# Layer three's mask added by GpSimd for six heads of sixteen, and a ring of six PSUM banks

## The chip, the cores and the metric

The kernel runs on one core of a Trainium2 chip. Five engines work side by side, each from its own queue in order: TensorE (PE in the profile: matmuls into PSUM; PEld its weight loads), VectorE (DVE), ScalarE (ACT), GpSimd (POOL) and SyncE (SP), which here issues every DMA. They meet only through semaphores. The time is the device time of one execution in microseconds (us), and lower is better.

## The reference

Sixteen sequences of 256 tokens with 256 features go through four residual steps. Layer zero is a low-rank spectral map; layers one, two and three are attention layers of 16 heads with 16 features each. Cut to what the change touches, layer three is:

```python
q, k, v = proj(Wq), proj(Wk), proj(Wv)
scores = jnp.einsum('bhsd,bhtd->bhst', q, k) * scale
scores = jnp.where(mask[None, None, :, :], -jnp.inf, scores)
attn = jax.nn.softmax(scores, axis=-1)
out = jnp.einsum('bhst,bhtd->bhsd', attn, v)
out = out.transpose(0, 2, 1, 3).reshape(B, S, E)
out = out @ Wo.T
rms = jnp.sqrt(jnp.mean(out * out, axis=-1, keepdims=True) + EPS)
xn = out / rms * rms_scale
mod = jax.nn.silu(conditioning) @ Wc.T + bc
shift, sc = jnp.split(mod, 2, axis=-1)
xn = xn * (1.0 + sc[:, None, :]) + shift[:, None, :]
...
x = x + _L3_cond_ref(x, mask_SxS_bk1, cond_256, ...)
```

Layer one adds a gated feed-forward net with 1024 hidden features behind its attention. Layer two multiplies the attention by a learned coherence and mixes a field in; it has no mask and no feed-forward net.

## The kernel before

The unit of work is a batch (one of the 16 sequences) of one layer. All of x stays in SBUF (`xres`). The order of each engine's queue is written out by numbers: `SLOT[layer]` gives every step of a batch a slot, a batch is 16 slots long (one for each head of the exponential pass), `LATER` shifts a step on one engine alone, and `schedule(engine)` sorts all steps of all batches of all layers by these numbers. So a batch's projections stand two batches ahead of its exponentials, its row maxima one batch ahead, and its output projection one batch behind. `run_layers` walks through that order on every engine.

The steps of a batch, with the names that the text below uses:

- **xT, q, k, v** (L1120, L1104, L1104, L1112): transposes and projections on TensorE. For q and k ScalarE writes a rounded high part `qk_hi` (L969) and VectorE the rest `qk_lo` (L523; L519 in layer two). SyncE copies both parts to the rows of `qs` and `ks` (**stack** 0 to 3: q and k of heads 0 to 7, then q and k of heads 8 to 15).
- **smax h** (s0 to s15, L1183): scores of head h with queries in the rows, into one bank. VectorE takes each row's maximum: L541 in layers one and two, in layer three the clearing of `tick` (L535) and two passes that also add the mask (L538).
- **neg u** (neg0 for heads 0 to 7, neg1 for 8 to 15): VectorE turns the maxima into two rows, with two instructions over SBUF (L547, L549) and four transposes (L554). SyncE sends `nm` to two rows of `qs` (**max**).
- **probs h** (p0 to p15): scores with keys in the rows, less the maximum (L1193). In layer three a matmul of an identity with `big_k` (-1e30 where masked, else 0; L1191, 128x512 bf16) goes ahead of them into the same bank. ScalarE applies the exponential from the bank into a tile of `probs` in SBUF (L997). These tiles go round in a ring of 12, and one is free once the values of the head that used it are done.
- **pv g** (pv0 to pv3, four heads each, L1206): probabilities times values; pv0 with pv1 and pv2 with pv3 share a bank (a value group below). VectorE transposes the bank into `ot_raw` (L558), takes the reciprocal of the sums (**rz**, L568) and multiplies (**on**, norm, L573), then turns the result (**oT**, L583).
- **wo** (L1232): output projection into bank 7. In layer three ScalarE takes squares (**squares**, L1013), GpSimd the inverse root (`inv3`, L831, L836, L838), VectorE scales and writes `y` (**resid**, L622), GpSimd adds it to x (L793).
- **mod**: TensorE writes shift and scale of the batch to bank 7 (L1264, 128x512 bf16), VectorE copies them to `x_in` (L613), GpSimd adds the shift to x (L788).

The other seven banks are one ring (`Ring`): each use takes the next bank, and TensorE waits at a use until the reader of the use seven places earlier is done. The value groups are uses of this ring too:

```python
head = middle = back = Ring(sem("banks_full"), banks[0:7])
```

The order of the steps is that of `schedule("tensor")`, and so is the order of the banks. "Batch of layer three" below means 16 slots of the table.

## Time and profile before

| | us |
|---|---|
| median of 3 runs | 1528.32 |
| lowest, highest run | 1528.09, 1529.13 |
| the profiled execution | 1526.98 |
| its span, first to last instruction | 1525.2 |

| engine | busy, us | share of the span | instructions |
|---|---|---|---|
| TensorE, matmuls | 1445.9 | 95% | 10235 |
| TensorE, weight loads | 1199.9 | 79% | 10283 |
| VectorE | 1094.8 | 72% | 3688 |
| ScalarE | 711.7 | 47% | 1555 |
| GpSimd | 264.5 | 17% | 322 |

A busy share is a mean over layers that differ. Matmuls are pipelined and the profile models their ends, so the distance between two starts tells more than a duration. The idle time before an instruction names what ended it, as far as the profile shows. A 256-column fp32 matmul stands in the trace as two records, so four matmuls of a projection are eight records.

### The profile page before, as it was taken

Reading aid. Unit: us, or ns where it says so; the run is one execution under the profiler, and the core shown is the slowest. Engines: PE = TensorE matmul, PEld = TensorE weight load, DVE = VectorE, ACT = ScalarE, POOL = GpSimd, SP = SyncE. Lnnn points to the kernel's source line nnn. Section 1 sums busy time; section 2 is a strip of 40 time slices with the busy share of each in tenths; the row PEclk is TensorE's granted clock in tenths of the full one; section 3 lists DMA queues with packets and bytes.
Section 4 is the critical chain, followed back from the end, with each engine's and each line's share of the span. In section 5 each row is a group of like instructions: output and inputs, shape, how many; then the busy total and the mean of one; then the engine's idle time right before and its main releaser. Section 6 shows DMA issues by size and latency. Waiting matters only on the chain.

```text
span 1525.2 us, 29475 instructions
## 1 busy us (share of the span) xinstructions
PE 1445.9 (95%) x10235; PEld 1199.9 (79%) x10283; DVE 1094.8 (72%) x3688; ACT 711.7 (47%) x1555; POOL 264.5 (17%) x322
## 2 busy tenths in 40 slices
PE   2669999999999999999999999999999999999997
PEld 1457888888888888888888787887877878887885
DVE  7747666666666666665666767777678888898886
ACT  1336333434444444333435555555555555555554
POOL 7401000000000000000112232322321111111112
PEclk9879999999999999999999999999999999999999
DMA  7056233332223232222224546354463454564450
GB/s 284 1 75 90 40 50 50 50 49 44 43 37 50 50 50 44 38 58 39 43 43 78 74 61 79 56 73 73 58 83 65 77 94 79 78 93 82 78 90 22
DMA packets 101132, 100.00 MB, mean 66 GB/s; under 512 B 11494, under 2 KB 97640, under 8 KB 100346
## 3 DMA queue, kind: packets, MB, share of 16 engines
q1 hardware_dynamic: 100986, 98.14, 38.8%
q8 instruction: 82, 1.34, 0.5%
q14 instruction: 64, 0.52, 0.2%
HBM read 16.83 MB, written 4.19 MB: 14 GB/s over the span
## 4 chain that ended last, share of the span: by engine, by line
PE 84%; DVE 6%; DMA 5%; issue 2%; ACT 2%; SPq 1%; POOL 0%; ACTq 0%; DVEq 0%; POOLq 0%
PE bank L1245 15%; PE bank L1104 13%; PE bank L1193 11%; PE bank L1183 10%; PE bank L1206 10%; PE bank L1253 7%; PE bank L1232 5%; PE bank L1112 5%; DMA ks<-qk_lo 4%; PE bank L1191 3%; PE bank L1120 2%; DVE ot_raw L428 1%; DVE work L427 1%; ACT work L997 1%; SPq L681 1%
## 5 line engine op out<-in xcount | busy, mean ns | idle before, releaser
L997 ACT ACTIVATE work<-bank 128x512 f32<-128x512 f32 x768 | 450.2, 598 | 298.5 <-PE bank L1193 238.4
L541 DVE TENSOR_REDUCE rowmax<-bank 128x2 f32<-128x512 f32 x512 | 339.2, 679 | 121.4 <-PE bank L1183 121.2
L1193 PE MATMUL bank<-qs,ks 98*128 98x256 f32 x1536 | 411.8, 351 | 5.0 <-DVE rowmax L541 4.4
L1183 PE MATMUL bank<-ks,qs 96*128 96x256 f32 x1536 | 321.1, 291 | 10.7 <-DMA ks<-qk_lo 10.5
L1193 PEld LDWEIGHTS bank<-qs,ks 98*128 98x128 f32 x1536 | 274.0, 191 | 54.5 <-issue 11.5
L1183 PEld LDWEIGHTS bank<-ks,qs 96*128 96x128 f32 x1536 | 241.1, 190 | 24.6 <-DMA ks<-qk_lo 14.3
L538 DVE CUSTOM_DVE_ANT_0 c1t<-bank,big_q 128x256 bf16<-128x256 f32 x512 | 192.8, 421 | 0.7
L1206 PE MATMUL bank<-work,vp 128*32 128x256 f32 x3072 | 185.7, 382 | 0.0
L1023 ACT ACTIVATE work<-bank 128x256 f32<-128x256 f32 x128 | 49.1, 383 | 236.2 <-PE bank L1245 236.2
L1206 PEld LDWEIGHTS bank<-work,vp 128*32 128x32 f32 x3072 | 90.0, 109 | 65.4 <-issue 5.0
L1245 PE MATMUL bank<-yt,w_gate 128*128 128x256 f32 x512 | 131.8, 379 | 0.4 <-ACT yt L1017 0.3
L1253 PE MATMUL bank<-w_down,work 128*128 128x256 f32 x512 | 131.5, 379 | 0.0
L1245 PE MATMUL bank<-yt,w_hid 128*128 128x256 f32 x512 | 131.4, 379 | 0.0
L1104 PE MATMUL bank<-xt,wqkvo 128*128 128x256 f32 x512 | 121.2, 386 | 0.9 <-ACT xt L954 0.9
L1245 PEld LDWEIGHTS bank<-yt,w_hid 128*128 128x128 f32 x512 | 97.2, 190 | 13.3
L1104 PEld LDWEIGHTS bank<-xt,wqkvo 128*128 128x128 f32 x512 | 95.5, 193 | 13.6 <-ACT xt L954 1.7
L1245 PEld LDWEIGHTS bank<-yt,w_gate 128*128 128x128 f32 x512 | 91.2, 189 | 10.4 <-ACT yt L1017 1.0
L1253 PEld LDWEIGHTS bank<-w_down,work 128*128 128x128 f32 x512 | 91.2, 189 | 9.3
L596 DVE SCALAR_TENSOR_TENSOR work<-work,bank 128x256 f32<-128x256 f32 x128 | 53.3, 416 | 59.3 <-ACT work L1023 59.3
L554 DVE STREAM_TRANSPOSE nm<-negs 32x32 f32<-32x32 f32 x384 | 76.8, 200 | 12.3
L558 DVE STREAM_TRANSPOSE ot_raw<-bank 128x512 f32<-128x512 f32 x96 | 66.6, 694 | 25.1 <-PE bank L1206 25.1
L1191 PE MATMUL bank<-big_k,ident_bf 128*128 128x512 bf16 x208 | 80.4, 386 | 1.3 <-DVE ot_raw L558 1.1
(220 smaller groups left out, 1751.2 us busy)
## 6 DMA issues: line engine op xcount, KB each, us to landing
qs<-qk_hi SPq DMA_DIRECT2D x192, 128.0 KB, 4.0
ks<-qk_hi SPq DMA_DIRECT2D x192, 128.0 KB, 3.7
qs<-qk_lo SPq DMA_DIRECT2D x96, 128.0 KB, 4.5
ks<-qk_lo SPq DMA_DIRECT2D x96, 128.0 KB, 4.3
xres<-in_x_t SPq DMA_DIRECT2D x4, 1024.0 KB, 9.0
x_in<-in_x SPq DMA_DIRECT2D x16, 256.0 KB, 2.8
out<-xres SPq DMA_DIRECT2D x15, 256.0 KB, 2.9
qs<-nm SPq DMA_DIRECT2D x96, 16.0 KB
```

The costliest lines, as they stand in the source:

```text
L538: a = dve.tensor_tensor_reduce(masked[:, k % 2, t, :], bank[:, t * S:(t + 1) * S], big_q[:, t, :], 1.0, 2 * BIG, ALU.add, ALU.max, rowmax[ ...
L541: a = dve.tensor_reduce(rowmax[:, :, k:k + 1], bank[:, :].rearrange("p (t s) -> p t s", t=TC), AX, ALU.max)
L554: dve.transpose(nm[k][:, part].bitcast(F32), negs[k][part].rearrange("p a h t -> p (a h t)").bitcast(F32)).then_inc(L.nm.sem, 1)
L997: act.activation(probs[:, place[n, b, k], :, :], bank[:, :].rearrange("p (c s) -> p c s", c=TC), ACT.Exp, scale=HD ** -0.5)\
L1104: m = pe.matmul(bank[:, c * S:(c + 1) * S], weights[:, i, c * P:(c + 1) * P], acts[:, i, :], start=(i == 0), stop=(i == DC - 1))
L1112: m = pe.matmul(bank[:, t * width:(t + 1) * width], acts[:, i, t * P:(t + 1) * P], weights[:, i, :], start=(i == 0), stop=(i == n_in - 1))
L1183: m = pe.matmul(bank[:, t * S:(t + 1) * S], qs[par][0:SCORE_ROWS, k, t * P:(t + 1) * P], ks[par][0:SCORE_ROWS, k, :], start=True, stop=True)
L1191: pe.matmul(bank[:, :], ident_bf[:], big_k[:, :, :].rearrange("p c s -> p (c s)"), start=True, stop=False)
L1193: m = pe.matmul(bank[:, c * S:(c + 1) * S], ks[par][0:SHIFTED_ROWS, k, c * P:(c + 1) * P], qs[par][0:SHIFTED_ROWS, k, :], start=(n != 3), ...
L1206: m = pe.matmul(bank[HW * i:HW * (i + 1), (k % 2) * S:(k % 2 + 1) * S], vp[par][:, c, DC * (j % HALF) + j // HALF, :], probs[:, place[n, b ...
L1245: m = pe.matmul(bank[:, j * S:(j + 1) * S], wt[:, c, k * P:(k + 1) * P], yt[:, c, :], start=(c == 0), stop=(c == DC - 1))
L1253: m = pe.matmul(acc_bank[:, t * D:(t + 1) * D], hm[:, k % HMBUF, t * P:(t + 1) * P], w_down[:, k, :], start=(k == 0 and t == 0), stop=(k = ...
```

## The change

The diff does five things.

1. In layer three the heads 0, 1, 2, 8, 9 and 10 (`k % HALF < BESIDE`, six of sixteen) get no mask matmul. ScalarE copies their scores from the bank to the tile in SBUF (in the place of the exponential), GpSimd adds `big_k` to the tile (**cap**, a new step), and ScalarE applies the exponential to the tile in place (**expo**, a new step). The value groups wait for it.
2. Layer three gets four more tiles for probabilities, in `w_down`, which nobody reads any more by then (`probs_tile`).
3. The ring has six banks. Bank 6 belongs to the value groups alone, each of which waits until the group before it has been transposed.
4. The copy of shift and scale (mod) goes from VectorE to ScalarE.
5. The tables of slots have other numbers in all three layers.

```diff
+MOST = 4
+BESIDE = 3
...
+        "max": (-6.13, 2.38), "xT": -26.55, "q": -23.59, "stack": (-24.46, -19.29, -15.9, -15.03), "k": -21.32, "v": -12.83,
+        "cap": -0.18, "expo": 2.6, "mod": 14.15, "oT": 16.94, "wo": 20.71, "squares": 22.54, "resid": 23.94},
...
+        elif what in ("cap", "expo"):
+            out += [(at + h, what, h) for h in range(H) if h % HALF < BESIDE]
...
+def beside(b, k):
+
+    return b * DC * BESIDE + k // HALF * BESIDE + k % HALF
...
+            if (n, b) == (3, 0):
+                ring = list(range(PBUF + MORE, PBUF + MORE + MOST)) + ring
```

The changes to the ring, the tiles and the value groups, and the new steps:

```diff
-        head = middle = back = Ring(sem("banks_full"), banks[0:7])
+        head = middle = back = Ring(sem("banks_full"), banks[0:6])
...
-                if what == "pv":
-                    return [(head, f"pv{k // 2}", self.o_raw, k // 2 + 1)] if k % 2 == 0 else []
...
+        def probs_tile(n, b, h):
+
+            i = place[n, b, h]
+            return probs[:, i, :, :] if i < PBUF + MORE else w_down[:, TC * (i - PBUF - MORE):TC * (i - PBUF - MORE + 1), :]
...
+                    if what == "cap":
+                        tile = probs_tile(n, b, k)
+                        pool.wait_ge(L.probs.sem, L.probs.at(b, k + 1))
+                        pool.tensor_tensor(tile, tile, big_k[:, :, :], ALU.add).then_inc(beside_ok.sem, 1)
...
-                        act.activation(probs[:, place[n, b, k], :, :], bank[:, :].rearrange("p (c s) -> p c s", c=TC), ACT.Exp, scale=HD ** -0.5)\
-                            .then_inc(L.probs.sem, 1)
+                        tile, scores = probs_tile(n, b, k), bank[:, :].rearrange("p (c s) -> p c s", c=TC)
+                        if n == 3 and k % HALF < BESIDE:
+                            act.copy(tile, scores).then_inc(L.probs.sem, 1)
+                        else:
+                            act.activation(tile, scores, ACT.Exp, scale=HD ** -0.5).then_inc(L.probs.sem, 1)
...
+                        act.wait_ge(mod_full.sem, mod_full.at(b, 1))
+                        act.copy(x_in[:], acc_bank[:, :].rearrange("p (a d) -> p a d", a=2)).then_inc(mod_ok.sem, 1)
+                    if what == "expo":
+                        tile = probs_tile(n, b, k)
+                        act.wait_ge(beside_ok.sem, beside(b, k) + 1)
+                        act.activation(tile, tile, ACT.Exp, scale=HD ** -0.5).then_inc(beside_exp.sem, 1)
...
-                        if n == 3:
+                        lowered = n == 3 and k % HALF >= BESIDE
+                        if lowered:
                             pe.matmul(bank[:, :], ident_bf[:], big_k[:, :, :].rearrange("p c s -> p (c s)"), start=True, stop=False)
...
+                        if k % 2 == 0 and not (n == 1 and b == 0 and k == 0):
+                            pe.wait_ge(L.o_raw.sem, L.o_raw.at(b, k // 2))
                         pe.wait_ge(L.probs.sem, L.probs.at(b, HG * (k + 1)))
+                        if n == 3:
+                            pe.wait_ge(beside_exp.sem, beside(b, HALF * (k // 2)) + min(HG * (k % 2 + 1), BESIDE))
```

What the tables do to the queues is shown at three places. The numbers behind the names are those of buffers; the lines of the changed kernel are other ones (L1218 is the mask, L1220 the scores of probs, L1209 those of smax, L1130 q and k, L1234 the values).

**TensorE, a batch of layer three, around its k.** Before, from k's projection to smax9:

```order
L1104 MATMUL bank1<-xt,w_hid 128x256 x4
L1191 MATMUL bank2<-big_k,ident_bf 128x512
L1193 MATMUL bank2<-qs0,ks0 128x256 x2
L1183 MATMUL bank3<-ks1,qs1 128x256 x2
L1206 MATMUL bank4<-work,vp0 32x256 x16
L1191 MATMUL bank5<-big_k,ident_bf 128x512
L1193 MATMUL bank5<-qs0,ks0 128x256 x2
L1183 MATMUL bank6<-ks1,qs1 128x256 x2
L1191 MATMUL bank0<-big_k,ident_bf 128x512
L1193 MATMUL bank0<-qs0,ks0 128x256 x2
```

After, from smax8 to smax11:

```order
L1209 MATMUL bank0<-ks1,qs1 128x256 x2
L1130 MATMUL bank1<-xt,w_hid 128x256 x4
L1218 MATMUL bank2<-big_k,ident_bf 128x512
L1220 MATMUL bank2<-qs0,ks0 128x256 x2
L1209 MATMUL bank3<-ks1,qs1 128x256 x2
L1218 MATMUL bank4<-big_k,ident_bf 128x512
L1220 MATMUL bank4<-qs0,ks0 128x256 x2
L1209 MATMUL bank5<-ks1,qs1 128x256 x2
L1218 MATMUL bank0<-big_k,ident_bf 128x512
L1220 MATMUL bank0<-qs0,ks0 128x256 x2
L1209 MATMUL bank1<-ks1,qs1 128x256 x2
```

k stood behind smax6 and ahead of p9 and of the first value group; it now stands behind smax8. Its bank is bank 1, which comes round again at the last row, smax11.

**VectorE at the same place.** Before, from smax7 to the first transposed value group (k's low part in row six):

```order
L535 MEMSET tick 1x1
L538 ISA c1t,rowmax<-bank0,big_q 128x256
L538 ISA rowmax 128x1
L538 ISA c1t,rowmax<-bank0,big_q 128x256
L538 ISA rowmax 128x1
L523 TENSOR_TENSOR qk_lo<-bank5,qk_hi 128x512
L547 TENSOR_SCALAR negs0<-rowmax 128x16
L549 SCALAR_TENSOR_TENSOR negs0<-rowmax,negs0 128x16
L554 STREAM_TRANSPOSE nm0<-negs0 32x32 x4
L558 STREAM_TRANSPOSE ot_raw<-bank1 128x512
```

After, from the group's reciprocal of sums to k's low part:

```order
L583 RECIPROCAL rz<-ot_raw 128x16
L550 MEMSET tick 1x1
L553 ISA c1t,rowmax<-bank3,big_q 128x256
L553 ISA rowmax 128x1
L553 ISA c1t,rowmax<-bank3,big_q 128x256
L553 ISA rowmax 128x1
L538 TENSOR_TENSOR qk_lo<-bank1,qk_hi 128x512
```

k's low part is now taken behind the maxima of smax9 (bank 3), and no longer ahead of neg0 and of the value group.

**GpSimd, a batch of layer three.** Before, from one residual add to the next:

```order
L793 TENSOR_TENSOR xres<-xres,y 128x512
L788 TENSOR_TENSOR xres<-xres,x_in 128x512
L831 TENSOR_TENSOR statb<-statb,guard 128x2
L836 TENSOR_TENSOR statb<-statb,half 128x2
L838 TENSOR_TENSOR statb<-statb,some_key 128x2
L793 TENSOR_TENSOR xres<-xres,y 128x512
```

After (L796 is the new add, L805 the residual add, L800 the shift):

```order
L805 TENSOR_TENSOR xres<-xres,y 128x512
L796 TENSOR_TENSOR work<-work,big_k 128x512 x2
L800 TENSOR_TENSOR xres<-xres,x_in 128x512
L796 TENSOR_TENSOR w_down<-w_down,big_k 128x512 x3
L843 TENSOR_TENSOR statb<-statb,guard 128x2
L848 TENSOR_TENSOR statb<-statb,half 128x2
L850 TENSOR_TENSOR statb<-statb,some_key 128x2
L796 TENSOR_TENSOR work<-work,big_k 128x512
```

Two new adds stand between the residual add and the shift, three behind the shift, one ahead of the residual add.

**TensorE, a batch of layer two, around its k.** Before, from q's projection to the first value group:

```order
L1104 MATMUL bank1<-xt,wqkvo1 128x256 x4
L1104 MATMUL bank2<-xt,wqkvo1 128x256 x4
L1193 MATMUL bank3<-qs0,ks0 128x256 x2
L1183 MATMUL bank4<-ks1,qs1 128x256 x2
L1193 MATMUL bank5<-qs0,ks0 128x256 x2
L1183 MATMUL bank6<-ks1,qs1 128x256 x2
L1206 MATMUL bank0<-work,vp0 32x256 x16
```

After:

```order
L1130 MATMUL bank0<-xt,wqkvo1 128x256 x4
L1220 MATMUL bank1<-qs0,ks0 128x256 x2
L1209 MATMUL bank2<-ks1,qs1 128x256 x2
L1220 MATMUL bank3<-qs0,ks0 128x256 x2
L1130 MATMUL bank4<-xt,wqkvo1 128x256 x4
L1209 MATMUL bank5<-ks1,qs1 128x256 x2
L1234 MATMUL bank6<-work,vp0 32x256 x16
```

q and k stood side by side; the halves of heads p8, smax7 and p9 now stand between them. The value group has bank 6.

## Rows read from the trace of the kernel before

**Rows 1.** Busy time of each engine in one batch of each layer.

```profile
core 0: us, PE busy (x) PEld busy (x) DVE busy (x) ACT busy (x) POOL busy (x), PEclk, DMA share, GB/s
340.00:381.24 41.24, 41.24 (x270) 35.41 (x269) 27.04 (x61) 16.94 (x40) 3.02 (x5) 1.00 0.25 46
928.00:951.88 23.88, 23.22 (x186) 18.94 (x185) 17.57 (x44) 13.49 (x29) 6.91 (x8) 1.00 0.51 69
1380.00:1402.74 22.74, 22.74 (x186) 18.46 (x185) 19.71 (x106) 12.31 (x25) 3.65 (x6) 1.00 0.54 90
```

**Rows 2.** Timeline of GpSimd: start, duration, instruction, idle time before it.

```profile
1379.31 1.28 POOL L793 TENSOR_TENSOR xres<-xres,y 128x512 f32<-128x512 f32 x1 [2.19 <-DVE y L622]
...
1402.05 1.28 POOL L793 TENSOR_TENSOR xres<-xres,y 128x512 f32<-128x512 f32 x1 [2.19 <-DVE y L622]
```

**Rows 3.** Timeline of TensorE in layer three.

```profile
1384.13 0.39 PE L1191 MATMUL bank<-big_k,ident_bf 128*128 128x512 bf16 x1
...
1384.84 0.39 PE L1264 MATMUL bank<-mod_parts,pick 128*128 128x512 bf16 x1
1385.07 0.38 PE L1191 MATMUL bank<-big_k,ident_bf 128*128 128x512 bf16 x1
...
1392.03 0.40 PE L1183 MATMUL bank<-ks,qs 96*128 96x256 f32 x2
...
1397.25 1.89 PE L1104 MATMUL bank<-xt,w_hid 128*128 128x256 f32 x8
1398.98 0.38 PE L1191 MATMUL bank<-big_k,ident_bf 128*128 128x512 bf16 x1
```

**Rows 4.** Timeline of TensorE in layer two.

```profile
957.62 3.62 PE L1104 MATMUL bank<-xt,wqkvo 128*128 128x256 f32 x16
...
967.34 0.51 PE L1193 MATMUL bank<-qs,ks 98*128 98x256 f32 x2 [0.32 <-DVE rowmax L541]
...
971.35 0.50 PE L1183 MATMUL bank<-ks,qs 96*128 96x256 f32 x2 [0.32 <-DMA ks<-qk_lo]
```

**Rows 5.** Timeline of VectorE in layer three.

```profile
1380.39 0.69 DVE L523 TENSOR_TENSOR qk_lo<-bank,qk_hi 128x512 fp32r<-128x512 f32 x1
1380.99 0.17 DVE L547 TENSOR_SCALAR negs<-rowmax 128x16 fp32r<-128x16 f32 x1
...
1382.23 0.66 DVE L558 STREAM_TRANSPOSE ot_raw<-bank 128x512 f32<-128x512 f32 x1
...
1392.56 0.06 DVE L535 MEMSET tick<- 1x1 f32 x1 [0.21 <-PE bank L1183]
...
1393.30 0.17 DVE L547 TENSOR_SCALAR negs<-rowmax 128x16 fp32r<-128x16 f32 x1
```

**Rows 6.** Timeline of ScalarE: the cast of k, and what released it.

```profile
1399.18 0.58 ACT L969 CAST qk_hi<-bank 128x512 fp32r<-128x512 f32 x1 [0.64 <-PE bank L1104]
```

**Rows 7.** Groups of GpSimd by line, setup: busy time, mean ns, idle.

```profile
L762 POOL TENSOR_TENSOR y<-y,mod_parts 128x512 f32<-128x512 f32 x1 | 1.2, 1155 | 5.1 <-ACT mod_parts L910 5.1
```

**Rows 8.** Timeline of VectorE at two passes over SBUF.

```profile
1492.14 0.66 DVE L547 TENSOR_SCALAR negs<-rowmax 128x16 fp32r<-128x16 f32 x1
...
1511.09 0.70 DVE L573 TENSOR_TENSOR on<-ot_raw,rz 128x256 f32<-128x256 f32 x1
```

**Rows 9.** Timeline of GpSimd at the same two places.

```profile
1491.48 1.28 POOL L793 TENSOR_TENSOR xres<-xres,y 128x512 f32<-128x512 f32 x1 [1.05 <-DVE y L622]
...
1510.23 1.28 POOL L793 TENSOR_TENSOR xres<-xres,y 128x512 f32<-128x512 f32 x1 [1.05 <-DVE y L622]
```

**Rows 10.** Timelines of ScalarE and GpSimd: first square, last step to inv3.

```profile
1397.71 0.38 ACT L1013 ACTIVATE yn<-bank 128x256 f32<-128x256 f32 x1
...
1399.67 0.20 POOL L838 TENSOR_TENSOR statb<-statb,some_key 128x2 f32<-128x2 f32 x1
```

**Rows 11.** Timeline of VectorE in layer two: row maxima in a row.

```profile
966.65 2.42 DVE L541 TENSOR_REDUCE rowmax<-bank 128x2 f32<-128x512 f32 x4
```

**Rows 12.** The page's DMA issues: count, KB each, median us to landing.

```profile
ks<-qk_lo SPq DMA_DIRECT2D x96, 128.0 KB, 4.3
```

48 lines of the change are left out of this document (20 added, 28 removed).

## Prediction

> **What bounds the kernel now.** I read first the busy time by stretch, one steady batch of each layer [rows 1]. In layer one TensorE is busy for the whole 41.24 us of a batch, in layer three for the whole 22.74 us. The batch of layer three is dated by GpSimd's residual add, which comes at 1379.31 and again at 1402.05 [rows 2]. In layer two TensorE has 0.66 us of plain idle in 23.88 us, and its starts hide more. VectorE, the next engine, is at 66%, 74% and 87%; ScalarE at 41 to 56%, GpSimd at 7 to 29%. So the time is TensorE's queue plus what stops it. All of TensorE's work is at full clock (1.00, the 2.4 GHz level) in these stretches, and the change does not make it idle longer, so the clock is left out.
>
> Second I read starts, since ends of matmuls are modelled. In layer three a head with its mask (mask, its score matmuls, the next head's) goes from 1384.13 to 1384.84, 0.71 us; the 128x512 bf16 matmul alone (the same shape as a mask) from 1384.84 to 1385.07, 0.23 us [rows 3]. So a head without a mask takes 0.48 us. Eight records of a projection take 1.73 us (1397.25 to 1398.98) [rows 3].
>
> In layer two I add the same prices up from the start of q (957.62) to smax0 of the batch after next (971.35), 13.73 us [rows 4]: q and k 3.46, 19 halves of heads at 0.24 (p8 to s14, p0, s15, p1) 4.6, two value groups at 1.9 each, and 0.3 for the turns between kinds of matmuls, 12.1. **About 1.6 us of each batch there is waiting** for two things: VectorE's row maxima (967.34, released by rowmax) and the landing of k's rows (971.35, released by the transfer of qk_lo). The price 1.9 is an estimate: 22.74 less 16 x 0.71, four projections at 1.73, 0.46 for the transposes and 0.23 for mod, halved.
>
> **The change, part by part.** The sum is made against the profiled execution, 1526.98 us (span 1525.2); the median of the runs is 1528.32, and I add the difference of 1.3 at the end.
>
> *Masks removed.* Six heads in each of 16 batches lose the mask matmul: 96 x 0.23 = 22 us, or 1.35 us of a batch. As layer three has no gap on TensorE, all of it is on the path, if nobody else is late. Bounds: 0 where VectorE sets the pace, 1.35 where it doesn't. The next parts say who is late.
>
> *k in layer three.* Its projection now stands behind smax8, and VectorE takes k's low part behind smax9; there are six banks, and smax11 falls on k's. On TensorE smax11 is wanted 1.18 us after smax9 (p12 0.47, s10 0.24, p13 0.47). On VectorE the pass over smax9 starts 0.58 us after the matmul's start (1392.03, then the clearing of tick at 1392.56, which takes 0.05) [rows 3, 5], so 0.34 after its 0.24 us, and lasts 0.69 (to 1393.30) [rows 5]. Then qk_lo takes 0.61 (1380.39 to 1380.99) [rows 5] and I allow 0.08 for the semaphore: 1.72. **TensorE waits 0.54 us** in each of the 14 batches that have such a k. ScalarE's half isn't late: the cast starts 0.20 us after the projection and ends at 0.78 [rows 6], before smax9's maxima.
>
> *GpSimd beside VectorE.* Six adds of 128x512 per batch, each between 1.16 us (with a bf16 operand, L762) and 1.28 us (L793) [rows 2, 7]: I take 1.2, 7.2 us on top of 3.65 of 22.74 [rows 1]. GpSimd has the time. But VectorE's negs pass over SBUF took 0.66 us at 1492.14, while GpSimd's add ran from 1491.48 to 1492.76, and 0.17 us at 1380.99; a normalisation (on, two inputs in SBUF) that began at 1511.09 under the add of 1510.23 took 0.70 us and ended 0.28 us after it [rows 5, 8, 9]. Each batch has six such passes (two of negs with two instructions each, two of on). Where do they meet adds? The residual starts when inv3 is there. The squares start about 2.45 us behind wo's end on TensorE, inv3 is 2.16 us later (1397.71 to 1399.87) [rows 10], and from there VectorE has resid 0.8, smax6 0.69, q 0.61, smax7 0.69 ahead of neg0: it comes at about 7.5 us. GpSimd has cap8 at 4.6 to 5.8, the residual add to 7.1, cap9 to 8.3, cap10 from 8.4, all back to back. So the first negs pass hits cap9 and waits 0.6 to 0.9 us, and the second may hit cap10 and wait 1.2 more. From neg0 to k's low part there are 1.24 (1380.99 to 1382.23), 0.62, 0.69, 0.2, 0.69 and 0.61, in all 4.05 us [rows 5], so k's part would be done at 11.55 without a block, and smax9 lets it be done at 11.75 in any case. Slack 0.2: the block adds 0.4 to 0.7 us on the path, at the far end 1.9.
>
> The Trainium skill, SBUF — State Buffer, section "Who interferes with whom", says that a VectorE instruction in a two-port mode or with two SBUF inputs and a GpSimd instruction that reads SBUF exclude each other for a whole instruction, whichever came first; the trace agrees in the two rows above (0.66 and 0.70 us), and by this rule alone the second block comes too where cap10 is first.
>
> *Layer three's sum.* Per batch 1.35 less 0.54 less about 0.4 is a gain of 0.4 us; ends: 1.35 (nothing late) and -1.1 (both blocks). Times 14: 6 us, from 19 to -15. The last two batches have no projections to fill TensorE, so VectorE sets their pace; the very last gets two more steps ahead of its last value group (add 1.2, exponential 0.6): +1 us, from -2 to +3.
>
> *ScalarE.* Six more passes over 128x512 and the mod copy: 7 x 0.58 [rows 6] = 4.1 us on 12.31 of about 22 [rows 1]. It waits for cap0, cap1, cap2 in its queue with p3, p4, p5 behind them; but v, wo and xT (1.73, 1.73, 0.46) stand between those heads on TensorE, which covers about 1.2 us of lateness. I cost it at nothing; without that cover it would be up to 0.6 us a batch. VectorE loses the mod copy (0.6 us), which hides nothing on the path.
>
> *Layer two.* k moves behind p9, so neg0 (1.24 us) is done while TensorE works on k instead of piling up behind the first value group. In the kernel before, VectorE works at 0.6 us a reduction (966.65, four in 2.42 us) [rows 11] against 0.48 on TensorE, with neg0 in front. With the new order I get from the start of q: k's projection ends at 4.2, neg0 at 5.4, k's low part at 6.8, the value group at 6.5, smax9 at 8.0, smax10 at 9.1, and then 0.6 each. TensorE waits for smax10's maxima at s13 (0.4 us) and twice 0.1 to 0.2 after it; smax0 comes at about 12.95. The transfer of k's rows takes about 4.3 us from its issue [rows 12] and is issued near 7.4, so it lands at 11.7 and no longer counts. **Gain 0.8 us a batch**, in some 12 batches: 9.6 us, from 4 to 14.
>
> *Layer one.* The ring loses a bank, but value groups leave it. TensorE never waits there now [rows 1], and the feed-forward matmuls between heads give readers over 1 us; one answer, 0; up to 0.5 us in each of 16 batches if a reader is late.
>
> Sum: -6 +1 -9.6 = about -15: 1512 for the profiled execution, 1513 for the median.
>
> **The rivals.** (1) *Nothing late*: VectorE passes miss the adds and k is in time. For it: 13% of VectorE is idle in layer three. Against: the order of k. 1528.3 - 19 - 9.6 = 1500, and down to 1495.
> (2) *The end on the other side: both negs passes are blocked each batch.* GpSimd's chain of cap8, residual, cap9, cap10 takes the place of the masks: 2.4 us of waiting for 1.35 saved. It decides as soon as waiting passes 1.35 us a batch. Layer three then loses 15, layer two gains 4 to 10: 1528.3 + 15 - 10 = 1533 (1527 to 1540). For it: the adds are back to back. Against: a pass of 0.17 us may slip between two.
> (3) *Banks short in layer one*: 16 x 0.5 = 8 us of my gain are gone: 1521. Against: no wait there in [rows 1].
> (4) *The added work doesn't replace but only moves the load*, VectorE being at 87% [rows 1]: layer three is unchanged, layer two gains 4: 1524 to 1527.
>
> **How the numbers follow.** The forecast (1505 to 1519) 0.45, rival 1 0.13, rival 2 0.15, rival 3 0.15, rival 4 0.12. Within 0.2%, 1525.3 to 1531.4 (about what a measurement of this kernel can tell from no change), lie part of rivals 2 and 4: 0.12; slower than that 0.09; faster 0.79. The range from 1499 to 1529 leaves out the fast half of rival 1 and most of rival 2.
>
> **What would show it.** In the profile after: L1218 (mask) x160 at most; a steady batch of layer three of 21.9 to 22.5 us instead of 22.74; waits of score matmuls on VectorE's qk_lo at k's bank; L562 and L564 with durations over 0.6 us; layer two's batch at 23.1 instead of 23.88, with no wait on the transfer at smax0. A batch of layer three at 21.4 makes rival 1 true, one above 22.9 rival 2; waits in layer one make rival 3. I am wrong in the main step if layer two keeps 23.88.

## The result, and the profile after

| | before | after |
|---|---|---|
| median of 16 runs, us | 1528.28 | 1524.17 |
| lowest and highest | 1526.3 to 1529.8 | 1520.41 to 1527.45 |
| the profiled execution (its span) | 1526.98 (1525.2) | 1527.45 (1525.7) |

One run of before (1851 us) and one of e16 below (1648 us) are left out of the ranges and ratios as slow. The ratio is 0.9972, with a 95% interval from 0.9965 to 0.9979: the change gains 4.1 us, where 15 were forecast. The profiled execution of after is the slowest of its 16, so the traces differ by half a microsecond the other way. That is the first thing to read here: the runs of before lie within 4 us and those of after within 7, and those of after go with the granted clock (1520.41 us at 0.988, 1527.45 at 0.981; before 0.986 to 0.992 in the runs beside the experiments).

The busy times by stretch of after, which answer to [rows 1]: a steady batch of layers one, two and three, then four stretches where layers meet or end (behind the output projections of layer two's first and last batch, then from batch 13's to batch 15's in layer three). PEclk, the third value from the right, is the granted clock.

```profile
core 0: us, PE busy (x) PEld busy (x) DVE busy (x) ACT busy (x) POOL busy (x), PEclk, DMA share, GB/s
349.31:390.46 41.15, 41.15 (x271) 35.54 (x270) 26.75 (x62) 16.81 (x40) 3.03 (x5) 1.00 0.27 47
...
812.16:839.53 27.37, 26.08 (x186) 20.61 (x185) 17.68 (x44) 13.39 (x29) 6.91 (x8) 0.88 0.37 60
932.17:955.32 23.15, 22.93 (x186) 18.88 (x185) 17.47 (x44) 13.39 (x29) 6.91 (x8) 1.00 0.47 71
1181.31:1206.64 25.33, 23.56 (x176) 18.50 (x176) 20.87 (x107) 15.40 (x34) 10.62 (x12) 0.93 0.48 80
1318.90:1341.35 22.45, 21.85 (x175) 17.75 (x176) 19.84 (x107) 15.12 (x34) 10.59 (x12) 1.00 0.50 85
1476.25:1499.22 22.97, 18.16 (x142) 13.58 (x142) 19.22 (x99) 13.44 (x29) 9.73 (x12) 0.85 0.10 20
1499.22:1515.58 16.36, 11.11 (x103) 7.50 (x104) 7.08 (x17) 10.25 (x22) 8.10 (x9) 0.98 0.05 18
```

The steady batches came out as forecast: layer two 23.15 us (forecast 23.1, before 23.88), layer three 22.45 (forecast 21.9 to 22.5, before 22.75 by the same dates). Dated by the starts of the output projections, the time behind the setup (143.4 us before, 143.6 after) splits so, up to the end of VectorE's last instruction:

| stretch | before | after | difference | forecast |
|---|---|---|---|---|
| layer one, batches 0 to 12 | 535.17 | 534.06 | -1.1 | 0 |
| layer one, 13, to layer two, 1 | 180.75 | 185.06 | **+4.3** | about 0 |
| layer two, 2 to 12 | 263.48 | 254.70 | -8.8 | -8.8 |
| layer two, 13, to layer three, 0 | 88.20 | 89.26 | +1.1 | about -1 |
| layer three, 1 to 12 | 273.00 | 269.61 | -3.4 | -4.8 |
| layer three, 13, to the end | 39.10 | 47.31 | **+8.2** | +0.6 |

The forecast is the sum's own terms, dealt out (0.8 us for each batch of layer two, 0.4 for each of layer three, +1 for the end). What is missing isn't in the batches that were worked out. It stands at the three places where the steady pattern breaks (the two seams between layers, and the end), 13.6 us, and part of it is TensorE's clock. Behind the setup, the records of the granted clock show half (the 1.2 GHz level) from 825.3 to 832.1, 1197.3 to 1200.8 and 1487.5 to 1494.3 us in after, none there in before, and half from 1514.8 to the end (before: from 1522.4).

TensorE at the first of these places, with the idle time before a row and what ended it. First the waits, then score matmuls that take 0.43 us from start to start instead of 0.24, since the clock is at half:

```profile
769.83 0.40 PE L1209 MATMUL bank<-ks,qs 96*128 96x256 f32 x2
772.49 0.66 PE L1146 MATMUL bank<-ident,yn 128*128 128x128 f32 x4 [2.26 <-DVE yn L606]
...
778.05 1.13 PE L1271 MATMUL bank<-yt,w_gate 128*128 128x256 f32 x4 [0.82 <-ACT yt L1043]
...
823.09 0.51 PE L1220 MATMUL bank<-qs,ks 98*128 98x256 f32 x2 [0.89 <-DVE qk_lo L534]
...
826.18 0.63 PE L1209 MATMUL bank<-ks,qs 96*128 96x256 f32 x2
826.61 0.63 PE L1220 MATMUL bank<-qs,ks 98*128 98x256 f32 x2
```

In before TensorE had k's projection of layer two to do ahead of these transposes, and waited 0.56 us for them; its later waits there were 0.16, 0.31 and 0.32 us. At the second seam, between the output projections of layer two's last batch and layer three's first, TensorE waits twice as well, and half clock follows; before had no wait there:

```profile
1195.01 0.39 PE L1218 MATMUL bank<-big_k,ident_bf 128*128 128x512 bf16 x1 [0.93 <-DVE rowmax L553]
...
1196.47 0.50 PE L1209 MATMUL bank<-ks,qs 96*128 96x256 f32 x2 [0.84 <-DVE qk_lo L538]
```

A steady batch of layer three has one wait, at smax11, for k's bank: TensorE first, then VectorE, whose low part of k stands behind smax9.

```profile
1332.75 0.50 PE L1209 MATMUL bank<-ks,qs 96*128 96x256 f32 x2 [0.60 <-DVE qk_lo L538]
```

```profile
1331.66 0.42 DVE L553 CUSTOM_DVE_ANT_0 c1t<-bank,big_q 128x256 bf16<-128x256 f32 x1
1332.01 0.08 DVE L553 DVE_READ_ACCUMULATOR2_ANT rowmax<- 128x1 f32 x1
1332.01 0.69 DVE L538 TENSOR_TENSOR qk_lo<-bank,qk_hi 128x512 fp32r<-128x512 f32 x1
```

The two passes of neg0 in that batch, and two of GpSimd's additions: the first pass is held up, the second falls into 0.38 us in which GpSimd waits for ScalarE's copy.

```profile
1328.17 0.50 DVE L562 TENSOR_SCALAR negs<-rowmax 128x16 fp32r<-128x16 f32 x1
1328.71 0.18 DVE L564 SCALAR_TENSOR_TENSOR negs<-rowmax,negs 128x16 fp32r<-128x16 f32 x1
```

```profile
1327.49 1.15 POOL L796 TENSOR_TENSOR work<-work,big_k 128x512 f32<-128x512 f32 x1
1329.02 1.16 POOL L796 TENSOR_TENSOR work<-work,big_k 128x512 f32<-128x512 f32 x1 [0.38 <-ACT work L1011]
```

In the last batch but one, VectorE, GpSimd and TensorE. The two negation passes (L562, L564), 0.66 [rows 8] and 0.17 us there before, take 1.10 and 1.08, each to the end of one of two additions of GpSimd:

```profile
1484.40 1.10 DVE L562 TENSOR_SCALAR negs<-rowmax 128x16 fp32r<-128x16 f32 x1
1485.54 1.08 DVE L564 SCALAR_TENSOR_TENSOR negs<-rowmax,negs 128x16 fp32r<-128x16 f32 x1
1486.65 0.90 DVE L569 STREAM_TRANSPOSE nm<-negs 32x32 f32<-32x32 f32 x4
1487.48 0.66 DVE L573 STREAM_TRANSPOSE ot_raw<-bank 128x512 f32<-128x512 f32 x1
```

```profile
1484.31 2.27 POOL L796 TENSOR_TENSOR work<-work,big_k 128x512 f32<-128x512 f32 x2
```

```profile
1489.01 0.80 PE L1209 MATMUL bank<-ks,qs 96*128 96x256 f32 x2 [3.36 <-DVE rowmax L553]
```

The Trainium skill, SBUF — State Buffer, section "Who interferes with whom", says that where a VectorE instruction in a two-port mode and one of GpSimd meet, whichever issues first keeps the shared pair of ports for its whole instruction and the other is blocked fully; it also names two SBUF inputs of VectorE as a case that contends with GpSimd's reads. The two rows agree: 1.10 us from 1484.40 ends at 1485.50 and 1.08 from 1485.54 at 1486.62, and the additions end at 1485.47 and 1486.58.

The last output projection of TensorE, before and then after. It runs wholly at half clock after the change and takes twice as long:

```profile
1516.87 1.96 PE L1232 MATMUL bank<-w_hid,ot 128*128 128x256 f32 x8 [2.18 <-DVE ot L583]
```

```profile
1515.58 3.75 PE L1258 MATMUL bank<-w_hid,ot 128*128 128x256 f32 x8 [2.16 <-DVE ot L598]
```

### The profile page after: what moved, and what is told of

Its sections match the earlier page's. It is cut to its first block, busy times and chain, and to the rows that moved or that the text cites. A ratio compares the mean times of both kernels' runs of the same rounds, so it can differ in the third digit from the quotient of the medians.

```text
span 1525.7 us, 29540 instructions
## 1 busy us (share of the span) xinstructions
PE 1433.8 (94%) x10155; PEld 1193.0 (78%) x10187; DVE 1095.5 (72%) x3672; ACT 755.4 (50%) x1667; POOL 375.7 (25%) x418
## 4 chain that ended last, share of the span: by engine, by line
PE 78%; DVE 13%; issue 5%; ACT 3%; POOL 1%; DMA 1%; SPq 0%; DVEq 0%; ACTq 0%; POOLq 0%
PE bank L1271 15%; PE bank L1209 11%; PE bank L1220 10%; PE bank L1234 10%; PE bank L1130 9%; PE bank L1279 7%; PE bank L1258 5%; PE bank L1138 5%; PE bank L1146 2%; DVE c1t L553 2%; DVE rowmax L556 1%; DVE qk_lo L538 1%; DVE ot_raw L443 1%; DVE work L442 1%; PE bank L1218 1%
## 5 line engine op out<-in xcount | busy, mean ns | idle before, releaser
L1013 ACT ACTIVATE work<-bank 128x512 f32<-128x512 f32 x656 | 381.6, 598 | 189.4 <-PE bank L1220 141.1
L556 DVE TENSOR_REDUCE rowmax<-bank 128x2 f32<-128x512 f32 x512 | 335.6, 677 | 120.4 <-PE bank L1209 120.4
L1220 PE MATMUL bank<-qs,ks 98*128 98x256 f32 x1536 | 398.3, 342 | 2.5 <-DMA qs<-nm 1.1
L1209 PE MATMUL bank<-ks,qs 96*128 96x256 f32 x1536 | 339.0, 303 | 21.3 <-DVE qk_lo L538 9.8
L1220 PEld LDWEIGHTS bank<-qs,ks 98*128 98x128 f32 x1536 | 270.4, 192 | 49.8 <-issue 19.1
L1209 PEld LDWEIGHTS bank<-ks,qs 96*128 96x128 f32 x1536 | 245.1, 191 | 45.3 <-DVE qk_lo L538 13.1
L1234 PE MATMUL bank<-work,vp 128*32 128x256 f32 x2816 | 174.7, 387 | 2.0 <-ACT work L1039 1.2
L1234 PEld LDWEIGHTS bank<-work,vp 128*32 128x32 f32 x2816 | 84.1, 111 | 61.9 <-issue 4.8
L1130 PE MATMUL bank<-xt,wqkvo 128*128 128x256 f32 x512 | 123.4, 384 | 1.3 <-ACT xt L966 0.9
L843 POOL TENSOR_TENSOR stat<-stat,guard 128x2 f32<-128x2 f32 x16 | 3.2, 199 | 457.1 <-ACT xn L960 457.1
L1130 PEld LDWEIGHTS bank<-xt,wqkvo 128*128 128x128 f32 x512 | 94.1, 193 | 12.8 <-ACT xt L966 1.3
```

The source lines that it names most:

```text
L556: a = dve.tensor_reduce(rowmax[:, :, k:k + 1], bank[:, :].rearrange("p (t s) -> p t s", t=TC), AX, ALU.max)
L1013: act.activation(tile, scores, ACT.Exp, scale=HD ** -0.5).then_inc(L.probs.sem, 1)
L1130: m = pe.matmul(bank[:, c * S:(c + 1) * S], weights[:, i, c * P:(c + 1) * P], acts[:, i, :], start=(i == 0), stop=(i == DC - 1))
L1209: m = pe.matmul(bank[:, t * S:(t + 1) * S], qs[par][0:SCORE_ROWS, k, t * P:(t + 1) * P], ks[par][0:SCORE_ROWS, k, :], start=True, stop=True)
L1220: m = pe.matmul(bank[:, c * S:(c + 1) * S], ks[par][0:SHIFTED_ROWS, k, c * P:(c + 1) * P], qs[par][0:SHIFTED_ROWS, k, :], start=not lowere ...
L1234: m = pe.matmul(pv_bank[HW * i:HW * (i + 1), (k % 2) * S:(k % 2 + 1) * S], vp[par][:, c, DC * (j % HALF) + j // HALF, :], probs_tile(n, b, ...
```

## The experiments

Sixteen kernels, e1 to e16, each beside runs of the kernel from before on the same chip. Times are medians; each kernel starts from the changed one (1524.2 us) unless the text says otherwise.

**One order on VectorE in layer three (e1).** The low part of k is taken ahead of smax9.

```
+KLATER = {"vector": 0.4}
-steps += [(at + slot + LATER.get(engine, {}).get(what, 0), n, what, k, b) for ...]
+steps += [(at + slot + (KLATER if (n, what) == (3, "k") else {}).get(engine, LATER...(what, 0)), n, what, k, b) for ...]
```

> The changed kernel, with VectorE taking k's low part of layer three ahead of the score maximum smax9 instead of behind it; nothing else moves on any engine. Theory A (what is left of TensorE's wait in a batch of layer three, 0.7 to 0.87 us at smax11, is k's bank coming free late because its reader stands behind smax9's two instructions): the wait at smax11 falls by 0.4 to 0.8 us in each of some 14 batches, a steady batch of layer three goes from 22.45 us to 21.7 to 22.0, the kernel from 1524.2 to 1513 to 1519. Theory B (VectorE is short of time in that stretch whatever its order, since GpSimd's additions hold it up): the wait only moves to the bank of smax9, the batch stays within 0.15 us of 22.45, the kernel at 1522 to 1525.

Measured: 1512.99 us, ratio 0.9907 (0.9893 to 0.9920). One swap in a queue gives 11 us by the medians, 10 by the ratios, more than the whole change did. The batch, and VectorE's k now ahead of smax9's two passes:

```profile
1331.68:1353.40 21.72, 21.72 (x175) 17.66 (x176) 19.69 (x107) 15.00 (x34) 10.62 (x12) 1.00 0.49 88
```

```profile
1344.10 0.63 DVE L541 TENSOR_TENSOR qk_lo<-bank,qk_hi 128x512 fp32r<-128x512 f32 x1
1344.65 0.42 DVE L556 CUSTOM_DVE_ANT_0 c1t<-bank,big_q 128x256 bf16<-128x256 f32 x1
```

TensorE is busy for all of the 21.72 us, and smax11's wait is gone: 0.73 us a batch. Theory A holds; so the forecast had the right wait at the right instruction, and had priced it at 0.54.

**No additions (e2).**

```
-pool.tensor_tensor(tile, tile, big_k[:, :, :], ALU.add).then_inc(beside_ok.sem, 1)
-act.wait_ge(beside_ok.sem, beside(b, k) + 1)
-act.activation(tile, tile, ACT.Exp, scale=HD ** -0.5).then_inc(beside_exp.sem, 1)
+act.wait_ge(L.probs.sem, L.probs.at(b, k + 1))
+act.activation(tile, tile, ACT.Exp, scale=1e-3).then_inc(beside_exp.sem, 1)
```

> The changed kernel without GpSimd's 96 additions: the second exponential waits for the copy alone, and is taken with a scale of 0.001, so the mask of these six heads and their exponential are left out of what is computed, while every instruction of ScalarE and of TensorE stays. Theory A (beside the wait of k, the additions stretch VectorE's instructions that share memory with them: 0.50 us instead of 0.17 for the first negation, 0.75 instead of 0.42 for the product with the reciprocal, 1.10 and 1.08 instead of 0.17 in the last batch but one): VectorE's negation falls back to 0.17 us, a steady batch of layer three loses 0.2 to 0.5 us, the last two batches 2 to 4 us, the kernel is at 1514 to 1520. Theory B (the additions run beside the path and cost nothing there): 1522 to 1525, with the batch within 0.1 us of 22.45.

Measured: 1515.82 us (0.9924, 0.9912 to 0.9937). Groups of VectorE by line in one steady batch (busy us, mean ns of one), the changed kernel first, then this one:

```profile
L588 DVE TENSOR_TENSOR on<-ot_raw,rz 128x256 f32<-128x256 f32 x2 | 1.2, 585 | 0.0
...
L562 DVE TENSOR_SCALAR negs<-rowmax 128x16 fp32r<-128x16 f32 x3 | 0.8, 276 | 0.0
```

```profile
L588 DVE TENSOR_TENSOR on<-ot_raw,rz 128x256 f32<-128x256 f32 x2 | 0.8, 422 | 0.0
...
L562 DVE TENSOR_SCALAR negs<-rowmax 128x16 fp32r<-128x16 f32 x2 | 0.3, 172 | 0.0
```

The batch falls from 22.45 to 22.29 only, a little under theory A's 0.2: the additions lengthen VectorE's passes, and 0.16 us of it reach TensorE, through k's wait. From batch 13's output projection to the end it is 42.8 us instead of 47.3.

**All masks by TensorE, in both orders on VectorE (e3, e8).** The copies, additions and second exponentials go; the first kernel keeps the changed order, the second has k first as well.

```
+def aside(n, b, k):
+    return n == 3 and k % HALF < BESIDE and False
-if n == 3 and k % HALF < BESIDE:     # ScalarE's copy, and likewise the steps cap and expo
+if aside(n, b, k):
-lowered = n == 3 and k % HALF >= BESIDE
+lowered = n == 3 and not aside(n, b, k)
```

> The changed kernel with the mask of all 16 heads added by TensorE as before the change; the tables, the ring of six banks and k's new place stay, the copies, additions and second exponentials of layer three are gone. Theory A (the step times of the trace: taking six masks away shortened TensorE's steps by only some 0.73 us a batch, because the mask's matmul costs 0.19 us in the middle of a run of score matmuls, 0.09 behind the values and nothing behind a projection; and the wait at smax11 gave most of it back): a steady batch of layer three is 22.6 to 23.0 us, the last two batches are about 4 to 6 us shorter than in the changed kernel, and the kernel is at 1520 to 1527. Theory B (the forecast's price, 0.23 us for each mask, 1.35 a batch): a steady batch of 23.3 us or more, the kernel at 1530 or more.

> All 16 masks by TensorE, with k's low part ahead of smax9 in layer three: beside the changed kernel with that one order alone (1513.0, batch 21.71) it differs by the six masks and nothing that waits. Theory A (a mask costs what the step times show: 0.19 us in a run of scores, 0.21 ahead of a projection, 0.09 behind the values, nothing behind a projection, about 1.04 us for the six): a batch of layer three takes 22.75 us, the kernel 1519 to 1523. Theory B (the forecast's 0.23 us each, 1.35 a batch): a batch of 23.06 us or more, 1524 to 1528.

Measured: 1530.83 us (1.0019, 1.0009 to 1.0028) and 1519.05 us (0.9945, 0.9931 to 0.9958). A steady batch of each:

```profile
1345.22:1368.67 23.45, 23.01 (x181) 18.54 (x183) 19.41 (x105) 12.49 (x28) 3.66 (x5) 1.00 0.49 81
```

```profile
1338.51:1361.25 22.74, 22.74 (x184) 18.48 (x183) 19.24 (x105) 12.49 (x28) 3.67 (x5) 1.00 0.51 82
```

The first has theory B's numbers, but not its reason: the wait for k at smax11 is there even without an addition (0.44 us of idle time), and the second kernel, which takes it away, is 0.71 us a batch shorter. In the second kernel six masks are worth 22.74 - 21.72 = 1.02 us, theory A. It also says that 8.5 us below before are to be had with all masks where they were, by the rest of the change and k first.

The expectation's split by place was misread, though (its step times begin at the score matmuls, so a mask behind a projection is counted in the projection's step). Step by step between the two kernels, a mask costs 0.22 to 0.23 us in a run of scores, 0.22 behind q's projection, and 0.12 to 0.13 behind the values; and with the masks gone smax11's step and the one before it are 0.12 us longer, with no releaser shown. From the start of a pair of value groups' second half to smax8, with the mask (first fence: 1.44 us) and without (second: 1.32):

```profile
1346.89 1.05 PE L1242 MATMUL bank<-work,vp 128*32 128x256 f32 x16
1347.87 0.39 PE L1226 MATMUL bank<-big_k,ident_bf 128*128 128x512 bf16 x1
1347.91 0.59 PE L1228 MATMUL bank<-qs,ks 98*128 98x256 f32 x2
1348.33 0.40 PE L1217 MATMUL bank<-ks,qs 96*128 96x256 f32 x2
```

```profile
1339.62 1.05 PE L1237 MATMUL bank<-work,vp 128*32 128x256 f32 x16
1340.60 0.50 PE L1223 MATMUL bank<-qs,ks 98*128 98x256 f32 x2
1340.94 0.40 PE L1212 MATMUL bank<-ks,qs 96*128 96x256 f32 x2
```

**The last two batches by TensorE, then the last alone (e4, e15).**

```
-    return n == 3 and k % HALF < BESIDE and False
+    return n == 3 and k % HALF < BESIDE and b < NBATCH - 2
```

> The changed kernel with the mask of the last two batches of layer three added by TensorE as before the change, and by GpSimd in the other 14. Theory A (the additions made the end longer: in the last batch but one both negations of VectorE take 1.1 us, and behind the wait that follows the granted clock is at half for 6.8 us; in the last batch the exponentials wait for the additions): the stretch from the last batch but one to the end is 5 to 8 us shorter, the half clock at 1487 us does not come, the kernel is at 1516 to 1519. Theory B (the end is longer because of the ring of six banks and the new tables): the end stays, with the two masks' own 1.5 us added, 1523 to 1526.

> The changed kernel with k's low part ahead of smax9 and the masks by TensorE in the last batch of layer three alone, so that GpSimd's additions stay in batch 14. From batch 13's output projection to the end it took 46.5 us with the additions in both and 39.8 with none. Theory A (in batch 14 the additions hold both negations up, 1.1 us each instead of 0.2, and half of the loss stands there): 42 to 44 us for that stretch, the kernel at 1508.5 to 1510.5. Theory B (the loss is all the last batch's, whose exponentials wait for the additions with nothing else to do): 39.8 to 41 us, the kernel at 1505.7 to 1507. Theory C (all of it is batch 14's): 45.5 us or more, 1511.5 to 1513.

Measured: 1517.59 us (0.9936, 0.9924 to 0.9949), theory A, with no half clock at 1487 us (the stretch is 8.4 us shorter, a little more than its 5 to 8). The second, built on k first, 1510.29 (0.9879, 0.9865 to 0.9892), theory A too. From batch 13's output projection to the end the traces show 46.5 us with additions in both batches and k first, 43.2 with batch 14's alone, and 38.9 (in the first) or 39.8 (e11 below) with none. The clock is in these numbers, and step by step it can be set apart. From batch 14's output projection to batch 15's it is 16.28 us with the last batch's additions and 14.02 without: 2.3 us of waiting, for second exponentials that stand ahead of the last values with nothing beside them. Behind that, 1.8 us more are the last output projection at half clock (3.75 us against 1.97). From batch 13's output projection to batch 14's it is 18.67 us without additions (e4), 22.28 with them and 3.4 us of half clock (e1), 23.03 with them and 6.8 us of it (e15, first line below). So 3.4 us of half clock cost 0.7 there, and by an estimate from these three the additions alone cost 2.9 us in batch 14.

The last output projection is at half clock for most of its time in all seven traces with second exponentials in the last batch (3.50 to 3.75 us). Of the eleven others, seven have it at full clock (1.96 to 1.97) and four partly at half (2.43 to 3.54), so the additions aren't its only cause.

```profile
1462.81:1485.84 23.03, 18.99 (x144) 14.08 (x145) 18.89 (x99) 13.37 (x28) 7.03 (x9) 0.85 0.11 21
1485.84:1499.86 14.02, 11.53 (x105) 7.78 (x107) 5.56 (x17) 6.82 (x17) 3.66 (x5) 1.00 0.06 21
```

**The seam of layers one and two: k back at one batch, then at all (e5, e6).**

```
-at + slot
+at + (-24.09 if (n, what, b) == (2, "k", 2) else slot)
```

> The changed kernel with one projection moved: k of batch 2 of layer two stands directly behind its q again, ahead of smax7, as before the change; all other batches of layer two keep the new place. Theory A (TensorE's wait of 2.4 us at the first batch of layer two, for the transposes of layer one's last batch, lies open since that projection no longer stands ahead of it, and the half clock that all the profiles with the new order show near 772 or 826 us follows it): the last batch of layer one and the first of layer two together take 69 to 71 us instead of 73 to 74.4, no half clock there, the kernel at 1518 to 1521. Theory B (only the wait is covered, and the clock falls there for another reason): 1.7 us, 1522 to 1523. Theory C (the projection covers nothing, since the wait moves behind it): 1523.5 to 1525.

> The changed kernel with layer two's k back at its old place, behind q, in every batch; the other new numbers of layer two's table stay. Theory A (the 0.73 us that a batch of layer two won come from k's new place, which puts the transfer of ks and the banks in time): a steady batch goes from 23.15 to 23.8 or 23.9 us, 8 us in all, less the 3 to 5 us at the seam of layers one and two: the kernel at 1526 to 1530. Theory B (they come from the other numbers: stack, negations, norm, the second pair of value groups): the batch stays at 23.15 and with the seam mended the kernel is at 1518 to 1521.

Measured: 1524.90 us (0.9973, 0.9962 to 0.9984) and 1540.60 (1.0084, 1.0071 to 1.0097). The first is a miss: theory C. TensorE in it:

```profile
772.08 0.66 PE L1146 MATMUL bank<-ident,yn 128*128 128x128 f32 x4 [0.55 <-DVE yn L606]
...
776.94 1.10 PE L1271 MATMUL bank<-yt,w_gate 128*128 128x256 f32 x4 [1.64 <-DVE qk_lo L534]
```

The wait of 2.26 us shrinks to 0.55 and comes back as 1.64 at the next step, for a bank that holds a projection. The chain from the output projection to the first feed-forward matmul (11.1 us before, 12.9 after, 12.2 here) sets that place. At the same 6.8 us of half clock the last batch of layer one and the first of layer two take 73.5 us here and 74.4 in the changed kernel, so the trace gives the edit 0.9 us, which the times don't show; why the chain stays longer than before is open. The second is beyond theory A: the batch of layer two goes to 24.11 us, 0.96 more than 23.15 and above the 23.88 of before. k's new place is the gain, and the other new numbers without it cost 0.2. Batches 2 to 12 take 12.2 us more than in the changed kernel's trace.

**Three edits together, then without the seam's (e7, e11).** Both have k first and the last two batches' masks by TensorE; the first also has k of one batch of layer two moved as above.

> The changed kernel with three edits together: k's low part ahead of smax9 on VectorE in layer three, the masks of the last two batches by TensorE, and k of batch 2 of layer two behind q. Theory A (the three losses stand at three places and add up): 1513.0 of the first alone, less 7.6 us of the end (46.5 us from the last batch but two to the end with the first edit, 38.9 with the second), less 3 to 4 us of the seam: 1500 to 1504, with a batch of layer three at 21.7 us. Theory B (what is mended at one place is lost at the next, since the granted clock falls wherever TensorE gets ahead): 1507 or more, with half clock at new places in the trace.

> The changed kernel with two edits: k's low part ahead of smax9 in layer three, and the masks of the last two batches by TensorE. Beside the kernel with the third edit (k of batch 2 of layer two behind q), 1507.7 us, it shows what that one is worth. Theory A (nothing: the wait for the transposes then comes back ahead of the first feed-forward matmul): 1506 to 1509. Theory B (it is worth the 1 to 2 us that its profile showed at the seam): 1508.5 to 1510.

Measured: 1507.68 us (0.9866, 0.9853 to 0.9879) and 1505.70 (0.9857, 0.9843 to 0.9870). The first has theory B's number, but not its reason: its batch of layer three is 21.70 us and its one half clock stands at the old place, 825 us; what is missing are the 3 to 4 us that theory A gave the seam. In the times that edit is worth nothing (theory A of the second, whose 1506 to 1509 was met to 0.3 us), though the same two batches take 72.1 us with it and 73.1 without, at 3.4 us of half clock each. The other two edits add up in full: 11.2 and 6.6 us alone, 18.5 together.

**The ring (e9, e14, e13).** The changed kernel with seven banks, the kernel of before with six, and seven banks with the two edits.

```
-        head = middle = back = Ring(sem("banks_full"), banks[0:6])
+        head = middle = back = Ring(sem("banks_full"), banks[0:7])
```

> The changed kernel with the ring of seven banks from before the change, the value sums drawing from it as then, instead of six and one bank kept for the values; tables and additions stay as changed. Theory A (the losses where the layers meet come from the smaller ring: TensorE waits for banks that VectorE and ScalarE still read): from layer one's batch 13 to the end of layer two's batch 1 the trace takes 181 to 183 us instead of 185.1 (180.8 before the change), and the kernel is at 1519 to 1522. Theory B (they come from the order of the new tables, which bring the steps to TensorE ahead of what they need): 184 to 186 us for that stretch, the kernel within 2 us of 1524.2; a steady batch of layer one stays at 41.15 in both.

> The kernel from before the change, with its tables and its 16 masks by TensorE, and one thing of the change: six banks in the ring and one kept for the values. Theory A (a smaller ring costs some 0.2 to 0.35 us a batch in layers two and three whatever the order): batches of 24.1 and 23.1 us, the kernel at 1533 to 1537. Theory B (it costs under the new tables alone, which had to be made for it and still lost): batches within 0.1 us of 23.88 and 22.75, the kernel within 2 us of 1528.3. Theory C (the old order needs the seventh bank much more, and the tables were new for that reason): over 1540.

> The changed kernel with the ring of seven banks, k's low part ahead of smax9 in layer three, and the masks of the last two batches by TensorE. Theory A (the ring's loss in layer two, 0.23 us a batch, and k's wait in layer three, 0.75 us, are two things; in layer three both edits mend the same wait, and beyond it TensorE is bound by its own work): batches of 22.92 and 21.70 us, the kernel 2.8 us and what the seam gives below 1505.7: 1500 to 1503. Theory B (with the banks dealt out anew, k's order on VectorE meets another reader): a batch of layer three of 21.9 us or more, 1504 or more. Theory C (the gains add up in layer three as well): a batch of 21.35, the kernel at 1498 or less.

Measured: 1513.41 us (0.9903, 0.9888 to 0.9918), 1528.77 (1.0004, 0.9996 to 1.0013), 1503.45 (0.9833, 0.9820 to 0.9847). The first has theory A's stretch (181.5 us), but neither of its theories had this: the steady batches are shorter, 22.93 instead of 23.15 in layer two and 22.10 instead of 22.45 in layer three, where the wait for k has moved one step on and shrunk. That is 6.7 us; the rest of the 10.8 stands mostly at the seams, where its trace has no half clock (181.5 us for the second row of the table above, instead of 185.06, and 87.0 for the fourth, instead of 89.26):

```profile
950.00:972.93 22.93, 22.74 (x187) 18.89 (x185) 17.45 (x43) 13.25 (x29) 6.92 (x8) 1.00 0.45 71
1331.06:1353.16 22.10, 21.74 (x177) 17.68 (x176) 19.71 (x107) 15.12 (x34) 10.60 (x12) 1.00 0.46 86
```

```profile
1344.91 0.39 PE L1220 MATMUL bank<-big_k,ident_bf 128*128 128x512 bf16 x1 [0.36 <-DVE qk_lo L540]
```

With the old tables the smaller ring costs nothing in layer two (23.88 us a batch) and 0.13 in most batches of layer three (22.88), just outside theory B's 0.1; the time shows no difference. With k first it costs nothing in layer three (21.70 with seven banks, 21.70 to 21.72 with six) and 0.23 in layer two. So in layer three ring and order are one wait: the order mends it whole and the ring half (theory A of the third, whose time was missed by 0.5 us). The third kernel is the fastest made here, 24.6 us below before.

**Eight heads aside instead of six (e12)**, on the two edits: `BESIDE = 4`.

> The kernel of the two edits with eight heads in sixteen masked by GpSimd instead of six, in batches 0 to 13 of layer three: heads 3 and 11 join. Theory A (TensorE alone sets the batch now; one of the two masks stands in a run of scores, worth 0.19 us, the other behind v's projection, worth nothing there, and the steps around gain a little): a steady batch goes from 21.70 to 21.3 to 21.5 us, the kernel 3 to 5 us below that of the two edits, 1502 to 1505. Theory B (two more additions of 1.16 us hold VectorE's instructions up until one of TensorE's banks is late again): a batch of 21.7 us or more, the kernel at 1507 or more.

Measured: 1537.37 us (1.0057, 1.0044 to 1.0070), theory B by a wide margin. VectorE's second negation in a steady batch, and the batch:

```profile
1349.97:1373.94 23.97, 22.03 (x175) 17.63 (x174) 21.52 (x105) 16.19 (x36) 12.87 (x14) 1.00 0.49 80
```

```profile
L572 DVE SCALAR_TENSOR_TENSOR negs<-rowmax,negs 128x16 fp32r<-128x16 f32 x2 | 2.3, 1126 | 0.1
```

It takes 1126 ns instead of 176: now both halves' second pass meets an addition in every batch, and TensorE waits 0.72 and 1.14 us for row maxima. This is the prediction's rival 2, one step of GpSimd further on: 2.27 us a batch for two heads more.

**Idle matmuls in TensorE's wait (e10, e16)**, ten on the changed kernel, four on the fastest one.

```
+                        if b == NBATCH - 1:
+                            for _ in range(10):
+                                pe.matmul(bank[:, 0:S], w_c1[:, 0, 0:P], w_c1[:, 1, :], start=True, stop=True)
                         pe.wait_ge(yn_ok.sem, yn_ok.at(b, 2))
```

> The changed kernel with ten idle float32 matmuls (0.2 us each) put into TensorE's wait of 2.4 us ahead of the transposes of layer one's last batch, in the bank that these transposes then overwrite. They compute nothing that is used. Theory A (the granted clock falls to half because TensorE stood still there; kept at work it keeps its clock): no half clock between 770 and 835 us, the last batch of layer one and the first of layer two take 71 to 72 us together instead of 72.1 to 74.4, the kernel is 1.7 to 3.4 us below the changed one, 1520.5 to 1522.5. Theory B (the clock falls there whatever TensorE does in that wait): half clock at 772 or 825 as in all other profiles of this order, 1523.5 to 1525. Theory C (the ten matmuls themselves make the wait longer): 1525 to 1527.

> The same as e13_ring7_two_mends, with four idle float32 matmuls (8 records of 0.22 us, 1.7 us together) in TensorE's wait of 2.4 us ahead of the transposes of layer one's last batch; ten such had kept the clock at full speed but took 4.2 us and made the wait 1.9 us longer. They compute nothing that is used. Theory A (the clock falls because TensorE stands still there): no half clock between 770 and 835 us, the kernel 0.5 to 2.5 us below e13_ring7_two_mends, with a smaller spread of its runs. Theory B (chance, or other waits): half clock there in this profile too, or no difference beyond 0.5 us.

Measured: 1523.16 us (0.9967, 0.9955 to 0.9980) and 1503.32 (0.9830, 0.9817 to 0.9843). The first time lies between theories A and B, the second is theory B's no difference. The ten were mis-sized: they are 20 records, 4.3 us, and put 1.9 us on top of the wait. Yet the stretch is shorter than in the changed kernel's trace (48.82 + 24.48 = 73.3 us against 74.4), as the clock stays at full:

```profile
764.30:813.12 48.82, 48.00 (x308) 41.17 (x307) 28.16 (x64) 17.38 (x42) 8.12 (x10) 1.00 0.29 61
813.12:837.60 24.48, 23.20 (x186) 18.96 (x185) 17.46 (x44) 13.38 (x29) 6.92 (x8) 1.00 0.43 67
```

Counted over all traces: in the 14 with the new order and no fill, 13 have half clock between 772 and 833 us (3.4 to 6.8 us long, three times at 772 to 777 alone, seven times at 823 to 833 alone, three times at both), and only e9 has none. The two with a fill have none, and neither have the two with the old order. That speaks for standing still as the cause, but it isn't shown. e9 has the same waits (2.25, 0.82 and 0.89 us) and no half clock, and e16 has e9's ring, so its profile says little. The times don't show it either: 1503.32 against 1503.45 is no difference, and 1523.16 against 1524.17 lies within the spread.

## Why the prediction was wrong in size

Sign and range were right, the time wasn't: -15 forecast, -4.1 measured. Three terms failed: the end, the seams, and the clock that was left out. Step by step:

**The end (+1, from -2 to +3): this is the step that failed most.** It was priced as two more steps ahead of the last values. It cost 8.2 us. Some 4.3 are batch 14's: both negations blocked (1.10 and 1.08 us), TensorE standing 3.36 us behind VectorE (2.9 us, an estimate from e1, e4 and e15), and half clock for 6.8 us (1.4, likewise). In the last batch 2.3 us are the wait for second exponentials, which was priced at about 1, and 1.8 the last output projection at half clock (3.75 us instead of 1.96). That is 0.2 more than the 8.2, as the new order without additions is 0.2 us shorter there than before. The prediction had this very mechanism as rival 2 for the steady batches, at up to 1.9 us, and didn't carry it to the batch without projections, where nothing on TensorE covers it. Without the additions (e2) the stretch is 4.5 us shorter; with masks by TensorE (e4) it is back at 38.9, the 39.1 of before.

**"The change does not make it idle longer, so the clock is left out."** It does make it idle, at all three breaks. The last batch of layer one and the first of layer two together take 71.2 us with no half clock (e9, with the seventh bank), 72.6 to 73.1 with 3.4 us of it (e1, e3, e11, e15, and e13 with the seventh bank) and 74.4 with 6.8 (after). With the ring of six the first batch of layer two alone takes 24.48 us at full clock (e10) and 27.37 with 6.8 us of half clock (after): 2.9 us. Layer two's last batch and layer three's first take 46.1 us with 3.4 of it (after) and 44.5 with none (e10, the same program there). At the end it is 1.4 and 1.8 us, as above. So in the trace of after the clock costs by this estimate 2.9 + 1.6 us at the seams and some 3.2 at the end, 7.7 in all. In the median of the runs it is less, since all others have a higher clock. The Trainium skill, TensorE: Matmul & The Clock Gate, Part 1, says that the throttled state is the default and activity releases it, and that the place of this release in a run of matmuls varies from run to run. The traces here show a variation of place for the fall, in the middle of a kernel: equal instructions up to layer three, half clock at 772 in some, at 825 in others.

**The seams** weren't worked out at all. Together they lost 5.4 us where a gain of 1 was forecast, and 4.5 of it is clock by the estimate above. The waits at the first are 2.26, 0.82 and 0.89 us against 0.56, 0.16 and 0.31 before. k's new place took from TensorE the work that stood in the first of them, but with k back most of the wait comes at the next step (e5), so what lengthened the chain is only in part shown. The rival "banks short in layer one" isn't it: its batch has no wait, 41.15 us.

**Masks removed (1.35 us a batch): mis-sized.** They are worth 1.02 (e8 against e1); six times the price of 0.23 is 1.38. The price of 0.23 came from the bf16 matmul of mod [rows 3], and is right in a run of scores and behind a projection (0.22 to 0.23); for the two that stand behind the values it is 0.12 to 0.13, and 0.12 us came back around smax11.

**k in layer three (wait of 0.54): right place, mis-sized.** It is 0.73 (e1), of which 0.16 is the additions' (e2) and 0.35 the missing seventh bank's (e9); the parts overlap. **GpSimd's block (0.4 to 0.7): too large**, 0.16. Its timetable was right: neg0 came 7.5 us behind the output projection's end, as forecast. But cap9 ran 0.3 us earlier than forecast and held the first pass up by 0.33 us only, and the second pass slipped through in GpSimd's 0.38 us of waiting; the forecast had the adds back to back. The three errors cancel: 1.02 less 0.73 is 0.29, near the forecast 0.4, and the trace shows 0.30. That the batch came out at 22.45 was luck. **The ring at no cost**: wrong under the new tables, 0.23 us a batch in layer two and 0.35 in three (e9).

**Layer two (0.8 us a batch): right**, 0.73, and no row there waits on a transfer any more. The one wait left is 0.18 us for row maxima. **Layer one (0)**: -0.09 a batch. **ScalarE (nothing)**: right in the steady batch, wrong in the last one.

Of the rivals, 1 (nothing late) is what e1 and e13 made true: a batch of 21.7, which the prediction put at 21.4. Rival 2 is true of the last batch but one, and of e12 throughout. Rival 4 has the measured time (1524 to 1527), but not its reason: layer three's steady batches did gain, and layer two's gained 8.8 us, not 4.

What stays open: why half clock comes at one of the waits in one run and at another in the next; whether the fill gains anything in time; and what makes the chain at the first seam longer than before.

## What to carry to other kernels

Work out the first and last batches of a pipeline apart from its steady one: a block of 1 us that the steady batch hides is open where the filler work ends, and the clock adds to the bill (3 of 8 us here). When a wait is found in a prediction, look at once at what one swap in the waiting engine's queue would do: here 10 to 11 us lay in it, and in layer three the ring's loss was the same wait. What an instruction costs depends on its neighbours, so take its price from the place from which it is removed.

## What the runs showed of the hardware

- A 128x512 bf16 matmul costs 0.22 to 0.23 us between score matmuls and 0.12 to 0.13 behind the value matmuls (e8 against e1).
- Two VectorE passes in a row can each be held up by one of two additions of GpSimd in a row (1.10 and 1.08 us instead of 0.17); which pass is hit turns on tenths of a microsecond (0.50 and 0.18 us in the steady batch, where GpSimd stood still for 0.38 us between two additions; 0.51 and 1.17 with eight heads aside, where it didn't).
- The granted clock fell to half within or behind waits of TensorE of 0.8 to 3.4 us in a kernel that is otherwise busy, for 3.4 or 6.8 us, and came back by itself; not each such wait had it. 6.8 us of it cost 2.9 us in a batch where TensorE is busy, and the eight records of an output projection took 3.75 us instead of 1.96.
- Ten float32 matmuls of 128x256 on 128 columns took 4.3 us, 0.216 us for each of their 20 records (e10).
